# The product with W_r moved out of the combining stage into a third stage beside the gathers, the combining stage written out step by step and storing one row per node

## The reference, cut to what matters

```python
xn  = layernorm(x)
agg = segment_sum(xn[src], dst) / max(counts, 1)
gnn = relu(agg @ W_l.T + b_l + xn @ W_r.T) + xn
x1  = x + gnn + mix(xn)                  # mix: attention, Wm, LN, 2-layer MLP, LN, + xn
z   = layernorm(x1);  y0 = z + x1        # kept for every node
w   = z @ wr + br                        # router weight, top 6249 nodes are picked
out = y0;  out[picked] += (gelu(z @ w1 + fb1) @ w2 + fb2) * w
```

## Time and profile before

| | |
|---|---|
| median of 3 runs | 2688.31 us (2688.16 to 2688.74) |
| profiled execution, its own time | 2688.11 us |
| its span, first to last instruction | 2686.4 us |
| PE busy | 2269.3 us, 84% |
| POOL busy | 1617.3 us, 60% |
| DVE busy | 1324.9 us, 49% |
| ACT busy | 958.1 us, 36% |
[...]

### The profile page before, as it was taken

How to read it: one execution, slowest core, us unless ns; L and a number is a source line. 1 busy time by engine, 2 the same in 40 slices (tenths; PEclk the granted TensorE clock), 3 DMA queues, 4 the chain that set the end, 5 groups by cost and what they waited for, 6 DMA issues and landing times.

```text
span 2686.4 us, 50791 instructions
## 1 busy us (share of the span) xinstructions
PE 2269.3 (84%) x13646; PEld 1880.8 (70%) x13647; DVE 1324.9 (49%) x3290; ACT 958.1 (36%) x2185; POOL 1617.3 (60%) x1719
## 2 busy tenths in 40 slices
PE   1299999988988898888888888888888999379998
PEld 1287777766776776676767776676766777269998
DVE  7644444443334334443444444545454788854444
ACT  7433333321222222222222222222222899235544
POOL 2577777777777777777777777777774000023332
PEclk7599999998888889989988999999999999579999
DMA  9766666664444444444444444444442899212221
GB/s 313 219 196 190 184 186 182 181 187 138 140 138 142 139 140 137 144 140 140 137 143 140 136 140 142 142 138 138 137 144 86 275 312 311 92 48 67 66 66 42
DMA packets 229947, 412.28 MB, mean 153 GB/s; under 512 B 38193, under 2 KB 129715, under 8 KB 229886
## 3 DMA queue, kind: packets, MB, share of 16 engines
q0 software_dynamic: 81296, 224.22, 29.2%
q1 hardware_dynamic: 147774, 186.59, 20.9%
q10 hardware_dynamic: 816, 0.79, 0.1%
HBM read 315.13 MB, written 96.32 MB: 153 GB/s over the span
## 4 chain that ended last, share of the span: by engine, by line
PE 35%; POOL 33%; issue 14%; DVE 12%; DMA 3%; ACT 1%; DVEq 1%; POOLq 0%
POOL gath_raw L631 32%; PE ps L1576 11%; PE ps L1410 5%; PE ps L1442 4%; PE ps L1365 4%; PE ps L1367 3%; DMA gath_raw<-xtab,srcI 2%; PE ps L1424 2%; DVE work L966 1%; DVE onehot L963 1%; PE ps L1452 1%; DVE onehot L950 1%; PE ps L1350 1%; PE ps L1484 1%; PE ps L1465 1%
## 5 line engine op out<-in xcount | busy, mean ns | idle before, releaser
L631 POOL DMA_INDIRECT gath_raw<-xtab,srcI x1563 | 1478.2, 946 | 476.4 <-issue 461.5
L1365 PE MATMUL ps<-gath_raw,onehot 128*128 128x256 f16 x1956 | 495.5, 289 | 197.8 <-DMA gath_raw<-xtab,srcI 106.7
L1367 PE MATMUL ps<-gath_raw,onehot 128*128 128x257 f16 x1956 | 497.7, 290 | 0.0
L778 DVE SCALAR_TENSOR_TENSOR onehot<-ps,blkbase,dstF 128x512 f32 x489 | 353.3, 746 | 262.2 <-issue 175.1
L1442 PE MATMUL ps<-work,w_s 128*128 128x256 f32 x1568 | 403.2, 415 | 0.7
L1365 PEld LDWEIGHTS ps<-gath_raw,onehot 128*128 x1956 | 199.7, 102 | 287.7 <-issue 254.0
L1442 PEld LDWEIGHTS ps<-work,w_s 128*128 128x128 f32 x1568 | 319.2, 209 | 49.5 <-issue 0.5
L852 DVE BATCH_NORM_STATS2 stats<-ps 128x6 f32<-128x256 f32 x196 | 74.4, 422 | 490.3 <-PE ps L1484 480.1
L1576 PE MATMUL ps<-split_raw 128*128 128x256 f32 x2376 | 292.7, 285 | 1.7 <-DVE split_raw L1076 1.5
L1576 PEld LDWEIGHTS ps<-split_raw 128*128 128x128 f32 x2376 | 287.8, 192 | 2.4 <-issue 1.9
L1193 ACT ACTIVATE work<-ps 128x512 f32<-128x512 f32 x98 | 58.5, 597 | 643.5 <-PE ps L1442 643.5
(11 more groups left out here) (204 smaller groups left out, 3157.4 us busy)
## 6 DMA issues: line engine op xcount, KB each, us to landing
work<-x_in SPq DMA_DIRECT2D x98, 256.0 KB, 3.7
ff_d<-work SPq DMA_DIRECT2D x49, 512.0 KB, 2.8
gath_raw<-xtab,srcI POOLq DMA_INDIRECT x1563
agg<-x_in SPq DMA_DIRECT2D x14, 896.0 KB, 7.2
xtab<-gath_raw SPq DMA_DIRECT2D x14, 896.0 KB, 4.9
xt_d<-work SPq DMA_DIRECT2D x49, 256.0 KB, 4.1
q_d<-work SPq DMA_DIRECT2D x49, 256.0 KB, 2.4
work<-q_d SPq DMA_DIRECT2D x49, 256.0 KB, 3.3
```

The source lines that it names most:

```text
L631: e.indirect_dma_start(out=gath[:, TPG * s + t, 0:2 * D], out_offset=None, in_=xtab[:, :], in_offset=bass.IndirectOffsetOnAxis(ap=srcI[:, ...
L778: v.scalar_tensor_tensor(out=onehots[:, ds(p % OHN * TPG, TPG), :], in0=ps[:, columns:columns + 1, 0:P].to_broadcast(shape), scalar=blkbas ...
L1365: t.matmul(ps[:, ds(BG + k % 2, 1), 0:D], oh, gath[:, r, 0:D], start=False, stop=False, skip_group_check=True)
L1367: last = t.matmul(ps[:, ds(BG + k % 2, 1), 0:AGW], oh, gath[:, r, D:2 * D + 1], start=False, stop=q == TPG - 1, skip_group_check=True)
```

## The change

- The edge groups are dealt out anew: two a step in the first stage, five (was six) in the second, and one a step in a new **third stage** `l_body` of 49 steps. All 1563 gathers stay, in the same order.
- In the second stage PE takes its first group ahead of the attention products of the step, not behind them. PE's loop there now holds six steps (was two), since the ring's slot repeats only after six.
- The third stage does, beside its group: load x turned (`xt_d`, 256 KB), eight products with W_r (`wrT`), one DVE operation that adds b_l on the way out of PSUM (`l_even`), store to `lin_d` (256 KB). The last steps of the second stage's MLP (`m_hidden`, `m_mlp_out`, `m_end`) move into its first two steps.
- The combining stage is written out, 49 steps without a loop on SP, DVE, ACT and PE. It loads `lin_d` in place of x turned. PE adds it by one product with the identity over 512 columns, then eight products with W_l, in a ring of four PSUM banks (was two). DVE: no bias addition, root and affine part for four blocks at a time, means and variances kept; the router's weight is the dot product of the row before its normalisation with wr, corrected once at the end for all nodes. ACT makes two scaled copies a step (was four): y0 alone, straight to `out`. `ff_d` is gone.
- Selection: four small operations `coefficients()` in its first round (mean, 1/(1/sigma + 1) times 1/sigma, router weight; stored as 16 bytes a node in `coef_d`), and indices for both tables.
- Feed-forward: per 128 rows POOL issues two gathers (y0 from `out`, 1 KB a row; coefficients, 16 bytes a row) in place of one; DVE rebuilds z from y0 (`f_norm`) ahead of the turn; the dot product there is gone.

The core of the diff:

```diff
-KG, MG = 2, 6
-NG = NSUP * (KG + MG)
+KG, MG, LG = 2, 5, 1
+NG = NSUP * (KG + MG + LG)
+GRING, GXRING, GBANKS = 4, 5, 4
+        GP = (BB, BC, BE, BF)
 SP
+            def l_io(i, s, j):
...
+                e.wait_ge(l_ps, i + 1)
+                if not (isinstance(i, int) and i >= NSUP - 2):
+                    l_load(i + 2, s)
+                e.wait_ge(l_ev, i + 1)
+                e.dma_start(rows(lin_d, 2 * i), llin[s]).then_inc(l_out[s], 16)
+            for i in range(NSUP):
+                if i + GRING < NSUP:
+                    e.wait_ge(g_s, i + 1)
+                    g_load(i + GRING)
+                if i >= 4:
+                    g_store(i - 4)
 DVE
+            def l_even(i, s, j):
+                e.wait_ge(l_ps, i + 1)
+                if past(i, 2):
+                    e.wait_ge(l_out[s], 16 * j)
+                v.tensor_tensor(llin[s], bank(BB + s), bcast(bl_s[:, :], 2), ALU.add).then_inc(l_ev, 1)
+            for i in range(NSUP):
+                g_sum(i)
+                if i % 2 or i == NSUP - 1:
+                    g_scale(i // 2)
+                g_dot(i)
+                if i % 2 == 0 and i > 0:
+                    g_affine(i // 2 - 1)
+            g_affine(NSUP // 2)
+            def f_norm(i, s, j):
+                n = 1 if isinstance(i, int) and i == FSTEPS - 1 else 2
+                e.wait_ge(f_in[s], 64 * j + 32 * n)
+                for u in range(n):
+                    last = v.tensor_scalar(frow[s][:, u, 0:D], frow[s][:, u, D:2 * D], fco[s][:, u, 0:1], fco[s][:, u, 1:2],
+                                           ALU.subtract, ALU.mult)
+                last.then_inc(f_ff, 1)
 ACT
+            for i in range(NSUP):
+                if i + 2 < NSUP:
+                    g_turned(i + 2, i % 2)
+                if i + 3 < NSUP:
                     e.wait_ge(g_T_ps, i + 2)
+                    g_means(i + 3, 1 - i % 2)
+                if i % 2:
+                    g_root(i // 2)
+                if i >= 3:
+                    g_out(i - 3)
 PE
-            steps(e, m_body, NSUP, 2)
+            steps(e, m_body, NSUP, RING)
+            def l_body(i, s6, j6):
+                s, j = s6 % 2, j6 * (RING // 2) + s6 // 2
+                seg(*l_place(s6, j6), *seg_values(e, mybir.EngineType.PE, (KG + MG) * NSUP + i, 1)[0])
+                if isinstance(i, int) and i == 0:
+                    e.wait_ge(m_ynT, NSUP)
+                    for h in range(2):
+                        m_hidden(NSUP - 1, (NSUP - 1) % 2, (NSUP - 1) // 2, h)
+                if isinstance(i, int) and i == 1:
+                    m_mlp_out(NSUP - 1)
+                e.wait_ge(l_x_in[s], 16 * j + 16)
...
+            def g_linear(i):
+                to = bank(GP[i % GBANKS])
+                e.wait_ge(g_in[i % GRING], 32 * (i // GRING) + 32)
+                if i >= GBANKS:
+                    e.wait_ge(g_s, i - GBANKS + 1)
+                t.matmul(flat(to), ident[:, :], flat(glin[i % GRING]), start=True, stop=False, skip_group_check=True)
+                e.wait_ge(g_aT, i + 1)
+                for u in range(2):
+                    for c in range(2):
+                        last = t.matmul(to[:, u, :], gaT[i % 2][:, c, u * P:(u + 1) * P], wlT[:, c, :],
+                                        start=False, stop=c == 1, skip_group_check=True)
+                last.then_inc(g_ps, 1)
```

More of the change, by code:

```diff
@@ new lines, in _, with g_store @@
+            steps(e, l_io, NSUP, 2, 3)
+            for k in range(2):
+                e.wait_ge(l_out[k], 16 * len(range(k, NSUP, 2)))
+            def g_store(i):
+                e.wait_ge(g_base, i + 1)
+                e.dma_start(rows(out, 2 * i), gbase[i % GRING]).then_inc(base_out[i % GRING], 16)
+            for i in range(NSUP):
[4 more added lines that the diff above has]
+                    g_store(i - 4)
@@ L577, in _ @@
+            for s in range(GRING):
+                e.wait_ge(base_out[s], 16 * len(range(s, NSUP, GRING)))
             for s in range(FSLOTS):
@@ L923, in _ @@
             own.link(v.tensor_scalar(rcnt[:, :], agg[:, :, D], 1.0, None, ALU.max))
[L924 to L932 removed]
+            v.reciprocal(rcnt[:, :], rcnt[:, :]).then_inc(agg_done, 1)
+            l_even(NSUP - 1, (NSUP - 1) % 2, (NSUP - 1) // 2)
+            v.tensor_reduce(gsum, wr_s[:, :], AX.X, ALU.add)
             for r in range(HALFD):
@@ new lines, in g_sum, with g_scale, g_affine @@
+                own.link(last)
+                for u in range(2):
+                    last = v.bn_aggr(gmv[:, 2 * i + u, :], ln_st[i % 2][:, u, :])
+                own.link(last)
+            def g_scale(q):
+                b = slice(4 * q, min(4 * q + 4, NBLK))
+                own.link(v.tensor_scalar(gve[:, b], gmv[:, b, 1], LN_EPS, None, ALU.add))
+                v.reciprocal(grc[:, b], gve[:, b]).then_inc(g_v, 1)
+            def g_affine(q):
+                b = slice(4 * q, min(4 * q + 4, NBLK))
+                e.wait_ge(g_f, q + 1)
+                v.scalar_tensor_tensor(out=gb[:, b], in0=gmv[:, b, 0], scalar=-1.0, in1=gf[:, b], op0=ALU.mult, op1=ALU.mult)
+                v.tensor_scalar(gg[:, b], gf[:, b], 1.0, None, ALU.add).then_inc(g_c, 1)
@@ new lines, in g_dot @@
+            def g_dot(i):
+                for u in range(2):
+                    last = v.tensor_tensor_reduce(out=gjunk[:, u, :], in0=gx1[i % GXRING][:, u, :], in1=wr_s[:, :], scale=1.0,
+                                                  scalar=0.0, op0=ALU.mult, op1=ALU.add,
+                                                  accum_out=gdot[:, 2 * i + u:2 * i + u + 1])
+                own.link(last)
+            own.at(base + 1)
+            for i in range(NSUP):
[5 more added lines that the diff above has]
+                    g_affine(i // 2 - 1)
@@ L993, in _, with coefficients @@
             v.tensor_copy(s_low, s_key)
+            def coefficients():
+                v.tensor_copy(gcoef[:, :, 0], gmv[:, :, 0])
+                v.tensor_copy(gcoef[:, :, 2], wtok[:, :])
+                own.link(v.reciprocal(gve, gg))
+                v.tensor_tensor(gcoef[:, :, 1], gf, gve, ALU.mult).then_inc(coef_set, 1)
             def search(keys, first):
@@ L1531, in _ @@
+            g_turn(0)
+            g_turn(1)
+            e.wait_ge(l_ev, NSUP)
+            g_linear(0)
+            for i in range(NSUP - 1):
+                if i + 2 < NSUP:
+                    g_turn(i + 2)
+                g_linear(i + 1)
+            e.wait_ge(s_tab_set, 1)
             for r in range(NDIG):
```

294 lines of the change are left out of this document (141 added, 153 removed).

## The result

| | before | after |
| --- | --- | --- |
| median us, 4 runs each | 2688.5 (2688.2 to 2690.6) | 2748.4 (2740.4 to 2755.5) |
| ratio to before | | 1.0222, 95% 1.0209 to 1.0236 |
| profiled execution, span | 2686.4 | 2753.8 |
| last gather starts | 2054.8 | 2197.5 |
| selection starts | 2300.92 | 2369.64 |

The change made the kernel slower, by 60 us, where I had forecast 69 us less. Nearly all of the miss is in one place: the gathers, whose last starts 143 us later, and which I had ending unchanged at 2055.7 us. From the last gather on the profiled execution is 75 us shorter than before, where I had forecast 69.

The account below looks back on a forecast made before the run. POOL's gathers were taken as the bound up to 2055.7 us, and DVE in the new combining stage. 2688.1 - 73.0 (combining stage with tail) + 1.1 + 3.1 = 2619.3, median 2619.5 us; range 2606 to 2632 us, chance 0.73.

Parts of the forecast that it names:

- The gathers pace the second stage: Second stage: PE's work fits the 25 us of a step's gathers, so they still end at 2055.7 us.
- the 1.7 us of other waits: Second stage: PE's idle time per step not named as a gather, taken from before and added to 23.1 us of work.
- PE's clock above 0.91: Second stage: with less waiting PE's granted clock stays above 0.91; named as a sign of being right.
- Loops: Code size: PE's six-step loop is about 1500 instructions, three times the old one; no row showed a loop that size.
- Rival 2: Second stage: PE needs 26.5 us a step, total 2692 us, chance 0.04; a third of it, 2644 us, 0.04.
- Rival 4: Second stage: waits named as gathers are PE's round trips with DVE and ACT; 28.5 us a step, 2791 us, chance 0.02.
- Third stage free: Third stage: PE's 3.3 us and DVE's 3.5 us a step hide beside the gathers' 5.0 us, at no cost.
- Tail: From the last gather to the combining stage: first means at 2066.7 us in place of 2084.2.
- Combining step 3.12 us on DVE: Combining stage: DVE is the bound, its step falling from 4.09 to 3.12 us; 53.1 us less in the stage.
- Selection +1.1 us: Selection: the coefficients operations add 0.8 us and two more index operations 0.3 us.
- feed-forward start +3.1: Feed-forward, ahead of its first turn: two more POOL issues and two DVE operations add 3.1 us, once.
- the third rival: Feed-forward: small gathers land over 1.4 us later, lengthening 23 steps; at 1 us excess 2642 us, chance 0.04.

Follow-up runs that it names:

- e7: after with PE's old order restored and 64 instructions that do no work put ahead of DVE's second-stage loop; 2610.3 us.
- e8: e7 with 56 added instructions for 64, and DVE loading the first group's three block numbers apart from the other twelve; 2610.8 us.
- e6: after with PE's old order restored (attention products ahead of a step's first group), DVE's code unchanged; 2618.0 us.
- f3: e7 with the identity product left out of the combining stage; ratio 0.9852 to before, in a batch where before took 3146 us.
- h3: after, in its new order, with 56 do-nothing instructions ahead of DVE's loop and DVE's load of block numbers split in two; 2612.0 us.
- h2: after, in its new order, with DVE's second stage written out as 49 steps without a loop, no instructions added; 2632.0 us.

## Why the prediction was wrong, point by point

- **The gathers pace the second stage: wrong, and the whole miss.** The failing step is "a step needs between 22.1 and 26.5 us; I take 23.1 plus at most 1.7 and let the gathers pace it". The row of PE's work was read well; what stood beside it failed. After, and then e7, over 1130 us that lie in the second stage of both:

```profile
650.00:1780.00 1130.00, 999.38 (x5426) 819.89 (x5425) 456.06 (x1159) 281.86 (x680) 766.52 (x811) 0.88 0.45 133
650.00:1780.00 1130.00, 1043.83 (x6195) 846.25 (x6193) 528.36 (x1334) 320.33 (x774) 854.59 (x905) 0.97 0.49 148
```

  At 20 gathers a step, e7 takes 25.0 us a step with PE busy 23.1, as sized. After takes 27.9 us: busy 24.6 at the lower clock, and idle 3.2. What failed was the 1.7 us of other waits, carried over from before, and with it the clock. The 1.7 us belonged to an order in which PE had products to run while DVE began a step. The change moved the first group ahead of them, and I costed that move at nothing, without naming what then stands in front of the first one-hot: a load of 1.6 to 3.4 us, visible in the trace of before in the queue of DVE, and whatever else holds DVE, which in after is the stop. The sign of being wrong that I had named came: 166.5 us of POOL waiting for `grp_used`. Between 1120.3 and 1407.5 us a step took 28.7 us (200 gathers, ten steps). The 22.1 us at the low end of the step were my estimate, and no run shows them: in e7 PE is busy 23.1 us, at clock 0.97.
- **"PE's clock above 0.91": wrong in after (0.88), right without the stops (0.97 in e7).** Behind the gap at 1549.5 us in after PE ran its products at clock 0.50, in 0.42 us for 0.27, so such a gap costs more than its length.
- **Loops: right for PE, DVE left out.** I weighed a fetch at PE's loop of six steps and found that the ring would cover it unless PE was late already. It came so: PE stands at its branch for 3.5 to 5.0 us on six passes in e7, and the gathers keep their pace. The stops that cost the time came on DVE, whose loop the change had shortened (five groups for six) and which I did not look at. In after the price is some 3.6 us a pass on DVE and 4.3 on PE, and the runs show that DVE's loop has it or not by where it lies.
- **Rival 2** had the place, PE not holding 25 us a step, and 0.08 in all. Its 26.5 us carried the same 1.7 us over, and so did not see the new wait either.
- **Rival 4** (28.5 us a step, 2791 us, with POOL idle on `grp_used`) had the size and the sign; its cause was not the right one: it had the waits named as gathers as PE's round trips with DVE and ACT already in before, while the waits that made the time are new and stand at the load and the stop of DVE. That after comes near its 28.5 us is chance. I gave it 0.02 since POOL never slowed in before; that row tells of the old order alone.
- **Third stage free: right** (161 gathers in 200 us).
- **Tail: -19.9 us forecast (first sum at 2072.2 us for 2092.1), too much by 2.6 to 8.** From the last gather's start to DVE's first sum are 22.8 us in after (2220.3 - 2197.5) and 21.0 in e8 (2075.3 - 2054.3), for my 17.4; e6 has 20.0 and e7 25.4. My own terms add up to 2066.0 us at the first means, not 2066.7 (2062.3 and 3.7), so the forecast should have been 0.7 us shorter still. In after the last rows landed 6.20 us behind the start of their gather, where I had 3.3 from a quiet row (0.95 and 2.3). SP sent eight transfers for the combining stage at the same time, and the last load of the third stage behind them; that these held the rows up was not tested. The 2.7 us that I gave the first eight products are an estimate that no run shows: in after they took 1.89 us at clock 1.00, while the turns ahead of them ran at 0.50, and the first sum stood 6.2 us behind the first means (2220.34 - 2214.15) for my 5.5:

```profile
2215.10:2217.00 1.90, 1.90 (x9) 1.81 (x10) 0.85 (x11) 1.49 (x4) 0.00 (x0) 0.50 0.41 138
2218.34:2220.23 1.89, 1.89 (x11) 1.63 (x10) 0.00 (x0) 0.00 (x0) 0.00 (x0) 1.00 0.00 0
```

- **Combining step 3.12 us on DVE: right in size (3.02), wrong in the bound.** I gave the identity product 0.43 us. It is fp32, stands as two records of 512 columns, and takes 0.86. So PE needs 3.02 and DVE, whose gaps closed better than I had read, 2.84 where PE does not hold it (f3). That the size came out near is luck: one engine was priced too high, the other too low. From the first sum to the selection the stage took 149.3 us for 155.7: 59.5 less than before, for my 53.1.
- **Selection +1.1 us, feed-forward start +3.1, step 11.94 unchanged: right.** From the selection's first operation to the first unbroken 96 products are 87.4 us (2457.09 - 2369.64); before 83.6 (2384.57 - 2300.92): +3.8 for +4.2. The small gathers are hidden and land sooner than I had them, 2.3 us behind their issue (median) and not 3.5, and the third rival is out:

```profile
agg<-coef_d,agg POOLq DMA_INDIRECT x49, 2.3
```

Taken together, the forecast of 2619.5 us is near what the change gives once its second stage is not held up: 2610.3 in e7 with the old order, 2612.0 in h3 with the new one, 0.3 to 0.4% below. Part of this is luck: the tail was forecast 7 to 8 us too short for these two, the combining stage 6 too long, and the 5.2 us at the end of the program stood in no term.

## What to carry to other kernels

When a change puts another instruction first in a stage or a step, ask what that one waits for on the other engine from the very start of its code: loads of registers and branches stand in no busy time, and only the queue rows show them. A stop at a branch can lie behind its record (DVE in after: 0.07 us of record, 3.6 us to the next instruction) or inside it (PE in after: a record of 4.3 us), so read both the record's length and the distance to the next one. Idle time that an engine had for other reasons may be carried over only if the order around it stays. When an engine stands with the releaser "issue", look at the branch instructions before you look at work, and test with instructions that do nothing: this kernel lost 4% by where a loop's code lies (2748.4 for 2641.9 us), with 22 stops at 0, 128 and 256 instructions added and none at 64, so a loop written out (h2, 2632.0 us), or an order that covers a stop (e6, 2618.0 us with its 22 stops), is safer than a lucky place.

## What was not expected of the hardware

- DVE's loop of 334 instructions (some 21 KB at 64 bytes each) stops at its branch with 0, 128 or 256 instructions added ahead (3.0 to 4.1 us in after), and not with 64, nor with 56 and a loop longer by 6. Before had a longer loop, of six groups, without stops. The rows would fit a period of 128 instructions, the 8 KB of one packet on that queue, but five places don't show one; which places are bad, and why before's longer loop was spared, stays open.
- PE's loop of six steps goes with 99 packets of 16 KB, 22 in before (69 for 1 between 700 and 1900 us), which I read as its code fetched again on every pass. Its branch takes 3.9 to 4.9 us in after, where that of before's loop of two steps takes 0.22, and it does so wherever DVE's stops come or go.
- In three of five batches all kernels, before too, took some 3100 to 3230 us. The first stage, alike in all kernels, ran there at clock 0.91 for 1.00, and engines stood in spans whose end the trace puts down to "remote", a sign that none of its own instructions gave (1614 us in e1 over all engines; none in the batches where before took 2688 us). Its cause was not looked into.
